# A new order of the first three blocks: staging homes for two matrices, loads held behind two gathers, POOL splitting two contexts

## The reference

```
x (4,512,512) f32, tokens (4,512) in 13..99985, ctx (4,512,512)
x = x + xattn(layernorm(x), tokens, ctx, ctx, ctx)
x = x + ffn(layernorm(x), router_w, wg, wu, wd)

xattn: expert = min(clip(token, 0, 24999) // 6250, 3)          # 4 experts
  g = silu(h @ ctx[e].T); u = h @ ctx[e].T; y = (g * u) @ ctx[e].T   # of the token's expert only
ffn: idx = argmax(x @ router_w.T)                              # 8 experts
  bitlinear(x, w) = act_quant(x) @ weight_quant(w).T   # 8-bit activations, weights in {-1,0,1}/s
  weight_quant: s = 1/mean|w|,  clip(round(w*s), -1, 1)/s
  y = bitlinear(relu(bitlinear(x, wg[e]))**2 * bitlinear(x, wu[e]), wd[e])
```

## Time and profile before

| | us |
|---|---|
| median of 3 runs | 268.2 (266.99 to 269.78) |
| the profiled execution | 267.64 |
| its span, first to last instruction | 265.9 |
| busy: PE, DVE, ACT, POOL | 236.1, 214.0, 212.8, 159.6 |
| chain that ended last, by engine | PE 72%, DVE 10%, issue 6%, POOL 5%, DMA 4% |
| mean granted TensorE clock | 0.985 |

### The profile page before, as it was taken

One profiled execution on the slowest core, in us unless ns is written; L12 is line 12 of the kernel. 1 busy time (PEld: TensorE's weight loads), 2 busy tenths in 40 slices (PEclk: granted clock), 3 DMA queues, 4 the chain that ended last, 5 costly groups with the idle time before them and its releaser, 6 DMA issues.

```text
span 265.9 us, 5805 instructions
## 1 busy us (share of the span) xinstructions
PE 236.1 (89%) x1413; PEld 173.5 (65%) x1423; DVE 214.0 (81%) x678; ACT 212.8 (80%) x324; POOL 159.6 (60%) x315
## 2 busy tenths in 40 slices
PE   2285868999999999999999999989969999999980
PEld 2133747888888888888888888877435555555530
DVE  5947898888887787878887887778869899989971
ACT  1886777698898788898888798886779999999960
POOL 4435014477778777767776766257826477556553
PEclk9997999999999999999999999999999999999996
DMA  5997339466654555684556653353257798311110
GB/s 210 429 409 284 137 158 355 159 235 212 220 202 126 198 210 222 255 296 153 211 208 223 210 207 108 160 161 106 110 182 259 251 301 290 119 41 65 60 41 0
DMA packets 13839, 51.72 MB, mean 195 GB/s; under 512 B 2862, under 2 KB 2862, under 8 KB 10224
## 3 DMA queue, kind: packets, MB, share of 16 engines
q1 hardware_dynamic: 8928, 37.91, 39.3%
q0 software_dynamic: 4880, 13.44, 14.3%
HBM read 40.49 MB, written 13.48 MB: 203 GB/s over the span
## 4 chain that ended last, share of the span: by engine, by line
PE 72%; DVE 10%; issue 6%; POOL 5%; DMA 4%; ACT 1%; SPq 0%; POOLq 0%; DVEq 0%
PE bank L1296 35%; PE bank L1397 17%; PE bank L1289 9%; PE bank L1369 5%; PE bank L1391 3%; DVE ctx_lo L828 2%; DMA x<-x_rows,gather 2%; DMA x_rows<-row,store_at 1%; POOL out_rows L529 1%; DMA late_rows<-x_rows 1%; POOL x L434 1%; DVE ternary L796 1%; DVE ternary L851 1%; PE bank L1315 1%; DVE stats L884 1%
## 5 line engine op out<-in xcount | busy, mean ns | idle before, releaser
L1397 PE MATMUL bank<-ternary,qT 128*128 x179 | 43.4, 379 | 0.4
L566 ACT ACTIVATE ternary<-staged 128x2048 bf16<-128x2048 f32 x22 | 42.0, 1910 | 1.2 <-DMA staged<-weight_chunks 1.2
L572 ACT ACTIVATE ternary<-staged,w_scale 128x1536 int16<-128x1536 f32 x22 | 34.5, 1566 | 3.3 <-DVE w_scale L840 3.3
L485 POOL DMA_INDIRECT x_rows<-row,store_at x19 | 25.0, 1314 | 15.6 <-DVE var_eps L892 8.5
L1397 PEld LDWEIGHTS bank<-ternary,qT 128*128 128x128 bf16 x184 | 17.7, 97 | 20.7 <-issue 4.6
L529 POOL DMA_INDIRECT out_rows<-late_rows x18 | 19.8, 1102 | 16.0 <-DVE late_rows L1140 14.3
L434 POOL DMA_INDIRECT x<-x_rows,gather x19 | 21.2, 1114 | 11.5 <-DVE row L934 6.0
L444 POOL TENSOR_TENSOR rstd<-var_eps,half_powers 128x1 f32<-128x1 f32 x19 | 12.5, 657 | 20.7 <-DVE var_eps L892 20.2
L600 ACT ACTIVATE pT_hi<-bank 128x512 fp32r<-128x512 f32 x19 | 11.3, 596 | 15.7 <-PE bank L1289 15.6
L1397 PE MATMUL bank<-ternary,rT 128*128 x87 | 22.6, 379 | 1.0 <-ACT rT L664 0.8
L1296 PE MATMUL bank<-ctx_hi,hT_hi 128*128 x76 | 22.5, 417 | 0.0
(11 more groups left out here) (213 smaller groups left out, 655.8 us busy)
## 6 DMA issues: line engine op xcount, KB each, us to landing
staged<-weight_chunks SPq DMA_DIRECT2D x22, 1024.0 KB, 5.5
late_rows<-x_rows SPq DMA_DIRECT2D x18, 260.0 KB, 3.3
ternary<-ctx_chunks SPq DMA_DIRECT2D x4, 1024.0 KB, 10.9
x_rows<-filler SPq DMA_DIRECT2D x9, 260.0 KB, 5.8
ternary<-weight_chunks SPq DMA_DIRECT2D x2, 1024.0 KB, 5.5
staged<-x_rows SPq DMA_DIRECT2D x5, 260.0 KB, 2.8
x<-x_rows,gather POOLq DMA_INDIRECT x19, 3.5
x_rows<-row,store_at POOLq DMA_INDIRECT x19, 3.4
```

Source lines behind the costliest of these rows:

```text
L485: pool.indirect_dma_start(x1_rows, bass.IndirectOffsetOnAxis(ap=store_at[b % ROWS][:, :], axis=0), row[b % ROWS][:, :], None, bounds_check ...
L566: nc.scalar.activation(ternary[:, m * K * D:(m + 1) * K * D], staged[i % 2][:, :], ACT.Abs, accum_out=abs_sum[:, 2 * i:2 * i + 1]).then_in ...
L572: nc.scalar.activation(ternary[:, m * K * D + DVE_COLS:(m + 1) * K * D].bitcast(I16), staged[i % 2][:, DVE_COLS:], ACT.Copy, scale=w_scale ...
L1397: last = pe.matmul(ps[:, :], left[:, k * P:(k + 1) * P], ternary[:, bass.ds(e * (3 * K * D) + (kind * K + k) * D, D)], start=(k == 0), sto ...
```

## The change

- SP loads matrices 2 and 3 into spare space of their own, and these two and contexts 2 and 3 only once POOL has issued `gather(1)` (`gathering` 2). Matrices 4 and 5 wait for the parts 0 and 1.
- POOL makes 3 of the 16 flag tiles and takes over the multiplication of `block_hot`; it makes `ctx_hi` of contexts 2 and 3 by copies, the first between `inverse_deviation(0)` and `gather(2)`, the second behind `gather(3)`.
- The block number is rounded by an integer tile, one instruction fewer; `gather1` is one instruction for two, ahead of the expert table (its lines moved, below in part).
- `normalise` only subtracts the mean; rstd is applied in `silu` and `gate`.
- VectorE makes ctx_lo in halves of 1,024 columns, at other places; the cuts of matrices 0 to 3 go to ticks 5 to 8.
- `first_product` of blocks 1 to 3 waits for the ctx_lo of its expert; block 0 waits by parts. The orders on ScalarE, VectorE and TensorE change as shown; the second warm-up has 5 matmuls for 8.

```diff
-WARM_UP = (4, 8, 4)
+WARM_UP = (4, 5, 4)
...
+        staged_early = [spare(8, 2 * K * D, F32), spare(10, 2 * K * D, F32)]
+        def staged_of(i):
+            return staged_early[i - 2] if i in (2, 3) else staged[i % 2][:, :]
...
-        POOL_TILES = TILES * 2 // 7
+        POOL_TILES = 3
...
             def load_weights(i):
-                if i >= 2:
-                    sp.wait_ge(dve_part, i - 1)
-                    sp.wait_ge(act_part, i - 1)
-                sp.dma_start(staged[i % 2][:, :], weights_in[ORDER[i]]).then_inc(staged_in[i % 2], 16)
+                if i in (2, 3):
+                    sp.dma_start(staged_of(i), weights_in[ORDER[i]]).then_inc(staged_early_in[i - 2], 16)
+                    return
+                if i >= 4:
+                    last = i - 4 if i < 6 else i - 2
+                    sp.wait_ge(dve_part, last + 1)
+                    sp.wait_ge(act_part, last + 1)
+                sp.dma_start(staged_of(i), weights_in[ORDER[i]]).then_inc(staged_in[i % 2], 16)
             load_context(0)
             load_weights(0)
             load_context(1)
             load_weights(1)
+            sp.wait_ge(gathering, 2)
+            load_weights(2)
             load_context(2)
+            load_weights(3)
             load_context(3)
-            for i in range(2, len(ORDER)):
+            for i in range(4, len(ORDER)):
                 load_weights(i)
-                if i == 2:
+                if i == 4:
...
+            wide = [P, TILES, B1]
             for t in range(POOL_TILES):
                 pool.tensor_scalar(row_hot[:, t, :], iota16[:, :], place_row[:, t:t + 1], None, ALU.is_equal)\
                     .then_inc(pool_hot_ready, 1)
+                if t == 0:
+                    pool.wait_ge(flagged, 1)
+                    pool.tensor_tensor(block_hot, block_hot, token1[:, :, None].to_broadcast(wide), ALU.mult)\
+                        .then_inc(blocks_hot_ready, 1)
...
+            def high_halves(e):
+                pool.wait_ge(ctx_in_sem[e], 16)
+                pool.tensor_copy(ctx_hi[:, e * K * D:(e + 1) * K * D], ctx_raw[e]).then_inc(pool_hi_ready, 1)
             def inverse_deviation(b):
                 if not 0 <= b < B1:
                     return
                 if b >= 2:
-                    pool.wait_ge(h_ready, b - 1)
+                    pool.wait_ge(p_ready, b - 1)
                 pool.wait_ge(var_ready, b + 1)
                 pool.tensor_tensor(rstd1[b % 2][:, :], var_eps[b % 2][:, :], half_powers[:, 0:1], ALU.pow)\
...
             gather(0)
-            pool.memset(fence[:, :], 0.0).then_inc(gathering, 1)
+            pool.memset(fence[:, :1], 0.0).then_inc(gathering, 1)
             gather(1)
+            pool.memset(fence[:, 1:2], 0.0).then_inc(gathering, 1)
             inverse_deviation(0)
+            high_halves(2)
             gather(2)
             inverse_deviation(1)
             gather(3)
+            high_halves(3)
             pool.wait_ge(tables1_ready, 1)
             for t in range(TICKS):
...
                     act.wait_ge(pT_ready, b)
-                nc.scalar.activation(p[:, :], a_ps[b % 2][:, :], ACT.Silu).then_inc(sil_ready, 1)
+                nc.scalar.activation(p[:, :], a_ps[b % 2][:, :], ACT.Silu, scale=rstd1[b % 2][:, :])\
+                    .then_inc(sil_ready, 1)
             def evict_x1T(b):
...
...
             high_halves(1)
             sum_abs(1)
             scale_part(0)
-            high_halves(2)
+            evict_hT(0)
             scale_part(1)
-            evict_hT(0)
-            high_halves(3)
             sum_abs(2)
             silu(0)
             evict_hT(1)
+            scale_part(2)
             evict_pT(0)
-            scale_part(2)
             sum_abs(3)
             silu(1)
...
                 square(t - 2)
-                scale_part(t + ABOVE)
+                if t > 2:
+                    scale_part(t + ABOVE)
                 silu(t)
                 evict_x1T(t - 2)
                 evict_hT(t + 1)
+                if t == 2:
+                    scale_part(t + ABOVE)
                 if t in EXTRA_SCALES:
...
-            link(dve.tensor_scalar(place_block[:, :], place_block[:, :], MAGIC, MAGIC, ALU.add, ALU.subtract))
             dve.scalar_tensor_tensor(place_row[:, :], place_block[:, :], -float(P), place[:, :], ALU.mult, ALU.add)\
...
-            link(dve.tensor_tensor(block_hot, iota[:, None, 0:B1].to_broadcast(wide),
-                                   place_block[:, :, None].to_broadcast(wide), ALU.is_equal))
-            dve.tensor_tensor(block_hot, block_hot, token1[:, :, None].to_broadcast(wide), ALU.mult)
+            dve.tensor_tensor(block_hot, iota[:, None, 0:B1].to_broadcast(wide),
+                              place_block[:, :, None].to_broadcast(wide), ALU.is_equal).then_inc(flagged, 1)
...
+            table_ps = bank[6][:, 0:B1]
+            dve.wait_ge(sort_pe, 2)
+            dve.tensor_scalar(gather1[:, :], table_ps, -1.0, 0.0, ALU.add, ALU.max).then_inc(sorted1, 1)
             wide = [P, B1, E1 - 1]
...
-            def low_halves(e):
-                cols = slice(e * K * D, (e + 1) * K * D)
-                dve.wait_ge(ctx_hi_ready, e + 1)
-                dve.tensor_tensor(ctx_lo[:, cols], ctx_raw[e], ctx_hi[:, cols].bitcast(F32),
-                                  ALU.subtract).then_inc(ctx_lo_ready, 1)
+            def low_half(e, part):
+                first = part * K * D // 2
+                cols = slice(e * K * D + first, e * K * D + first + K * D // 2)
+                if part == 0:
+                    dve.wait_ge(*((ctx_hi_ready, e + 1) if e < 2 else (pool_hi_ready, e - 1)))
+                ins = dve.tensor_tensor(ctx_lo[:, cols], ctx_raw[e][:, first:first + K * D // 2],
+                                        ctx_hi[:, cols].bitcast(F32), ALU.subtract)
+                if part == 1:
+                    ins.then_inc(ctx_lo_ready, 1)
             def mean_of(i):
...
...
             def normalise(b):
                 if not 0 <= b < B1:
                     return
-                dve.wait_ge(rstd1_ready, b + 1)
+                dve.wait_ge(moments_ready, b + 1)
                 if b >= 1:
                     dve.wait_ge(hT_ready, b)
-                dve.tensor_scalar(h[:, :], x[b % RING][:, :], moments[b % 2][:, 0:1], rstd1[b % 2][:, :],
-                                  ALU.subtract, ALU.mult).then_inc(h_ready, 1)
+                dve.tensor_scalar(h[:, :], x[b % RING][:, :], moments[b % 2][:, 0:1], None, ALU.subtract)\
+                    .then_inc(h_ready, 1)
             def hT_rest(b):
...
                 dve.wait_ge(sil_ready, b + 1)
-                dve.tensor_tensor(p[:, :], a_ps[b % 2][:, :], p[:, :], ALU.mult).then_inc(p_ready, 1)
+                dve.scalar_tensor_tensor(p[:, :], a_ps[b % 2][:, :], rstd1[b % 2][:, :], p[:, :],
+                                         ALU.mult, ALU.mult).then_inc(p_ready, 1)
             def pT_rest(b):
...
             dve.wait_ge(gathering, 1)
             mean_of(0)
             scale_of(0)
-            low_halves(0)
-            scale_part(0)
+            low_half(0, 0)
             moments_of(0)
+            aggregate(0)
+            normalise(0)
             variance(0)
             mean_of(1)
             scale_of(1)
-            normalise(0)
+            low_half(0, 1)
+            hT_rest(0)
             moments_of(1)
+            aggregate(1)
+            normalise(1)
             variance(1)
+            scale_part(0)
             scale_part(1)
-            hT_rest(0)
-            normalise(1)
-            cut(0)
-            low_halves(1)
             gate(0)
             hT_rest(1)
             mean_of(2)
             scale_of(2)
+            low_half(1, 0)
+            pT_rest(0)
             moments_of(2)
+            aggregate(2)
+            normalise(2)
             variance(2)
-            pT_rest(0)
-            normalise(2)
+            low_half(1, 1)
+            gate(1)
             scale_part(2)
-            cut(1)
-            low_halves(2)
-            gate(1)
             mean_of(3)
             scale_of(3)
+            hT_rest(2)
             moments_of(3)
-            hT_rest(2)
+            aggregate(3)
             variance(3)
             scale_part(3)
-            cut(2)
-            low_halves(3)
+            low_half(2, 0)
+            low_half(2, 1)
             early, factors = early_slots(), mean_products()
             for t in range(2, TICKS):
                 interlude = {EARLY_AFTER + 4: early, B1: factors}.get(t, iter(()))
                 residual(t - 2)
                 top_logits(t - 3)
                 negative_mean(t - 2)
-                mean_of(t + ABOVE)
+                if t > 2:
+                    mean_of(t + ABOVE)
                 if t in EXTRA_MEAN:
                     extra_mean(EXTRA_MEAN[t], t + ABOVE)
                 next(interlude, None)
                 choice(t - 3)
-                scale_of(t + ABOVE)
+                if t > 2:
```

(69 more changed lines are left out.)

13 lines of the change are left out of this document (8 added, 5 removed).

## The result

The changed kernel takes 283.17 us (median of 4, 282.05 to 284.44), the one before 267.93 beside it (median of 4, 266.99 to 269.78): a ratio of 1.056 with a 95% interval of 1.049 to 1.064. Forecast were 273.3 and at most 277. The profiled execution took 283.65, its span 281.9, the mean granted clock was 0.952 (before 0.985).

A forecast was written before the change was run, and what follows sets the result against it. The start was taken as VectorE-bound, the first layer from about 52 us as TensorE's. second_product(2) at 34.4 + 22.7 + 1.5 = 58.6 against 52.9 gave +5.7: 267.6 + 5.7 = 273.3 us, range 267.5 to 277.

The forecast's parts named there:

- the landing of x2: Block 2's rows, gathered behind POOL's copy of context 2: landing at 31.7, so first_product(1) starts at 34.4.
- the clock: TensorE idle 8 us before first_product(1): clock falls to half, 3 us of work at half speed, 1.5 us lost.
- the choice of the point: Shift summed at second_product(2), 52.89 before: everything behind it moves alike, as TensorE isn't idle until the layer ends.
- x0's statistics: VectorE's first work on block 0's rows: near 16.4, x0 landing 3.9 us earlier with loads held.
- x0's gather: First gather, with contexts 2 and 3 held back: 3.8 to 4.0 us to land, where it took 7.1.
- The gather list: gather1 on VectorE, behind the sort: written at 11.2 to 11.4, 0.5 to 1.2 us earlier.
- POOL's copy: Copy of context 2, 2,048 columns, ahead of gather(2): 2.7 us, between 2.1 and 5.8.
- From first_product(1) to second_product(2): Stretch of VectorE work and waits between the two products: 22.7 us, where it was 22.3.
- A: Rival: x2 comes in time, first_product(1) at 31.9, set by ScalarE; +3.2, 270.8 us; chance 0.22.
- B: Rival: VectorE's work from x0 to second_product(2) is what counts; -1.7, 265.9 us; chance 0.18.
- C: Rival: POOL's copies and VectorE hold each other off; first_product(1) up to 38.5, +9.8, 277.4 us; chance 0.10.
- the wait by expert: first_product waiting for its own expert's ctx_lo: saves nothing for blocks 1 and 2; already in the sum.

The follow-up runs named there:

- e2: Changed kernel with the first extra matrix's load issued one matrix later, behind matrix 6's: 278.21 us, 1.036 of the kernel before.
- e4: e3 with both halves of context 1's ctx_lo made ahead of scale_part(1) and gate(0) on VectorE: 267.22 us, 0.994 of the kernel before.
- e1: Changed kernel with gather(2) and gather(3) issued on POOL ahead of its copy of context 2: 279.29 us, 1.038 of the kernel before.
- e3: Changed kernel with the edits of both e1 and e2: 272.96 us, 1.018 of the kernel before.
- e10: e4 with 8 warm-up matmuls ahead of transpose_p(0): 266.58 us, 0.995 of the kernel before.
- e7: e4 with POOL's copy of context 3 moved behind inverse_deviation(2) and 8 warm-ups ahead of transpose_p(0): 268.62 us, 1.002 of the kernel before.
- e5: Changed kernel with 46 warm-up matmuls between transpose_p(0) and first_product(1): 280.57 us, 1.049 of the kernel before.
- e6: Changed kernel without SP's wait for the second gather, so all loads go out at once: 280.81 us, 1.048 of the kernel before.

## Why the prediction was wrong

The direction was right; of the 15.2 us lost, 5.7 were in the forecast and 9.5 weren't. Two things failed: the sum was closed at a point behind which more was lost (about 5), and up to that point the landing of x2 and the clock were priced too low (4.3 in all).

**The step that failed** is the choice of the point: "TensorE isn't idle behind it until the layer ends. The sum is made for it." It was true of the kernel before and not of the changed one. The prediction itself moved context 3's low halves behind first_product(2), and asked who on VectorE and TensorE would be later; it did not ask who else waits for ctx_lo 3. SP does, with the extra matrix's load and matrix 6's behind, which then went out together, and gather(5) fell among them. By the profile that is 4.8 us (14.9 at sp(3), 10.0 at sp(2)); e2 measured 5.0.

**Up to second_product(2)** the sum gave +5.7 and the trace shows +10.0:

- Right: x0's statistics (forecast 16.4, 16.80), first_product(0) (20.9, 20.40), x0's gather (3.8 to 4.0, 3.6). The gather list was no earlier than before (12.03, and 12.05 in the earlier trace rows), because three operations on the token numbers took 1.47 us instead of 0.71 in this execution; in e4 they took 0.67, and the list came at 11.3. From place_row on it is 3.67 us, not 4.27.
- POOL's copy: 1.89 us, and I had taken 2.7, with 2.1 as the lower end. A cost of 0.8 too much. The estimate of 1.8 from the Trainium skill (GPSIMD Engine Reference, 3.1) agrees with the row.
- Context 2 landed at 24.1, not 22.7 (0.7 of it because the held loads went out at 15.91, not 15.2), and gather(2) took 8.1 us, not 6.1 (7.1 was my upper end): together 3.4 too little. first_product(1) was 2.7 later than forecast. e1 and e4 bear the mechanism out: without copy and landing ahead of it, x2 is never waited for.
- The clock: 1.5 us for one product was forecast; it was 2.5 for first_product(1) and 1.6 for first_product(2), which followed a further 2.43 us of idle TensorE. 2.6 too little.
- From first_product(1) to second_product(2), leaving out the clock, 22.7 was forecast and 25.83 - 4.1 = 21.7 measured. (The pieces up to first_product(2) add up to 9.65, where the forecast has 9.45; measured, without the clock, are 9.55.)

2.7 + 2.6 - 1.0 = 4.3, the whole miss at this point. With it alone the time would be 277.6, just above the range.

**The rest.** Up to sp(3) 14.9 us are accounted for, and the profiled executions differ by 16.0. The granted clock fell once more far behind, in the second layer, to 0.50 from 194 to 196 us; in e2 and in the kernel before it did not there. Why it did is open.

**The rivals.** A (x2 in time, 270.8) needed a short gather; e3, where x2 is in time, took 272.96, with first_product(1) at 31.66 as A had it (31.9), but with both products cold. B rested on ctx_lo 1 being early, which is e4's edit: 267.2, and B gave 265.9. C's mechanism, POOL's copy and VectorE holding each other off, is real, costs 1.3 to 1.7 us where it strikes in full, and was not what cost the time here. Its end of 277.4 was the nearest, for another reason. That the wait by expert saves nothing for blocks 1 and 2 stays as read from the blocks' rows; no run tried it.

## What to carry to other kernels

When a producer is moved later, list every engine that waits on its semaphore, the DMA queue's own engine first: what stands behind that wait in the queue goes out later and closer together, and a small transfer issued just then pays for it (here two loads of 1 MB within 0.4 us, and 4.0 us for the gather behind them). Don't put a transfer on the critical path behind a computation that waits for another transfer (gather(2) behind high_halves(2)), and judge a hold on loads only once nothing on the path waits for the held ones. Pick the point at which a shift is summed up in the changed kernel's order, not the old one's.

## What the runs showed of the hardware

- An indirect gather of 128 rows of 2 KB took 3.6 us to land ahead of the loads, 3.9 two us behind a load of 1 MB with none following for 2 us (e2), and 7.9 with two such loads within 2 us ahead of it and one 2 us behind (gather(5)), 8.1 with several of them still under way (gather(2)); of four gathers in a row with loads behind them (e4) the slowest took 9.5.
- A VectorE operation with one input of 512 columns (the mean subtracted, or a part scaled), 0.48 to 0.49 us, took 1.80 to 2.17 when it started together with a POOL copy of 2,048 columns (1.89), or within 0.4 us behind its start, and 1.06 when it started 1.1 behind (e10). The Trainium skill (SBUF — State Buffer, Who interferes with whom) has such a `tensor_scalar` among the operations that can claim the shared ports, the later of the two waiting for the whole of the other instruction. The rows agree: in e4 it ends at 30.78 + 2.17 = 32.95, 0.28 behind the copy's end at 32.67, in e7 0.27 behind it, in e1 and e10 0.28.
- A product of 12 matmuls took 3.0 us at 2.4 GHz and 5.5 at 1.2. The clock was at the lower level for a product behind gaps of 11.4 us (the changed kernel) and 3.45 (e7). Behind gaps of 2.7 it was at the upper one in e5, e6 and e10, and at the lower one in e2 and e3 (2.07 for four matmuls). The length of the gap alone did not decide, nor did what the clock had been one product earlier: first_product(1) had been cold in e3 and in e6 alike. What decides is open.
